# One run of attention slots over four batches, ahead of a 512-step GRU

## The chip, the core and the metric

The kernel runs on one core of one Trainium2 chip. A core has five engines that run side by side: TensorE (PE, matrix products; its weight loads are shown as PEld), VectorE (DVE), ScalarE (ACT), GpSimd (POOL) and SyncE (SP, which here only starts transfers). Each engine takes its instructions in the order in which they are written; semaphores tie the engines together. The metric is the time of one execution on the device, in microseconds (us). Everything is float32.

## The reference, cut to what is computed

`x` is 4 batches of 512 rows by 512 features; `cond` is 4 by 512; there are 16 heads of 32.

```python
scale, shift = split(cond @ W_emb + b_emb)
xn   = rms_norm(x, g_norm) * (1 + scale) + shift
q,k,v = split(xn @ W_qkv)                      # 16 heads of 32
q, k = rms_norm(q, g_q), rms_norm(k, g_k)
o    = softmax(q @ k.T * 32**-0.5) @ v
x    = x + (o + o @ W_out)                     # the attention layer, added to x
hs   = GRU(cond, x): 512 wide, started from cond, one step for each position
x    = x + hs
```

In the GRU `r = sigmoid(..)`, `z = sigmoid(..)`, `n = tanh(i_n + r*h_n)`, `h = (1-z)*n + z*h`. The scan runs over the 512 positions, each step for the four batches at once.

## The kernel before

The program has two parts in time. First comes attention, one batch after another, then the input side of the GRU is begun, and then 512 GRU steps follow, which wait for each other. The diff touches the first part alone, and the way from it to the second.

**A batch of attention** (`for b in range(B)`, on every engine, L193 to L433 and L546 to L733) has four stages on TensorE. (1) The row transposes: the normed rows `xr` (four banks of 4 transposes, L327) and the raw rows `xb` (another four, L331) are transposed. DVE and ACT bring them out of PSUM as `xnT` (scaled and shifted by `mod_b`, L551 and L678) and `xT` (L557). (2) A run of `N_SLOTS` = 23 slots. In slot `s` the projection of tile `n = s` (q, k and v of one group of 4 heads and 128 rows, L355, 4 matmuls) stands beside the transposes of the normed q and k of tile `i = s - 2` (`transpose_qk`, L342) and beside the attention of "quad" `m = s - LAG` (4 heads, 128 query rows). There are 16 tiles and 16 quads, and LAG is 6. So slots 0 to 5 have projections alone, slots 6 to 15 have both, slots 16 to 21 have quads alone, and slot 22 ends the last quad. (3) The output projection of the batch (L430, 16 matmuls of 512 columns), from all of `oT`, the attention output, and `wout`. (4) The next batch.

**A quad in a slot**: TensorE makes the scores of 4 heads (L378) in the banks SC; DVE takes the row maxima (`negmax`, L701); ACT takes the exponentials (`probs`, L583) with their sums; TensorE transposes them (L416, 16 transposes, back into SC); DVE copies two heads and ACT two (`probsT`, L705 and L588); in the next slot TensorE multiplies them with `v_sb` (L392, "PV") into bank PO. The reciprocal sums, spread over the heads (`rexp`, L715), are transposed in the next slot (L351), copied by ACT (`rT_sb`, L578), and after four quads DVE multiplies them onto PO, which gives one group of `oT` (L721).

**The norms of q and k**: ACT squares the projected tile (`sq`, L566), DVE sums (`qk_ss`, L693), POOL adds, takes the power and spreads it (L282, L284, L286: `norm_qk`), DVE multiplies (`qn`, L687), and TensorE transposes `qn` into bank PM, from which ACT copies to `qkT` (L572).

**The ends of a batch**: POOL adds `oT` onto `xT` in one instruction of 128x2048 (L294), DVE adds the output projection in four parts (L733) into `x1T`, and signals `x1_ready`. After the last batch POOL clears half of the tile `seeds` (L297), and then starts the transfer of the GRU weights `whh` (L299). These lie in the place of `wqkv`, so it may start only when the last projection is done. DVE clears the other half and copies a bias into all of it (L725, L727). TensorE waits for `whh` and `x1_ready`, opens six banks (L468), and makes the first input-side products (`gi_piece`, L443). These go through DVE, SP and HBM before ACT seeds the first step.

The order of the work is written out by hand: it is the order of the code on each engine. In a full slot TensorE runs `transpose_qk(i)` first, then the transpose of `rexp`, then the four scores.

Of the kernel before, what the change touches and what calls it, by code (L numbers as in the profile page):

```python
# [28 lines left out]
ALU = mybir.AluOpType  # L29
ACT = mybir.ActivationFunctionType  # L30
# [4 lines left out]
P = 128  # L35
# [3 lines left out]
KT = D // P  # L39
# [8 lines left out]
N_SLOTS = N_QUADS + LAG + 1  # L48
# [11 lines left out]
def attention_gru_kernel(nc, x, cond, W_emb, b_emb, g_norm, W_qkv, g_q, g_k, W_out,  # L60
                         W_ih, W_hh, b_ih, b_hh, out):
    with ExitStack() as ctx:  # L62
# [20 lines left out]
        mod_b = sb("mod_b", [P, 2 * KT])  # L83
# [10 lines left out]
        xT = sb("xT", [P, KT, T])  # L94
# [31 lines left out]
        with ExitStack() as attention_only:  # L126
# [4 lines left out]
            xnT = attention_only.enter_context(nc.sbuf_tensor("xnT", [P, KT, T], F32))  # L131
# [10 lines left out]
        pj = lambda n: SC[n] if n < 4 else PJ[n % 2]  # L142
        X_BANKS = (PO, PJ[0], PJ[1], PM)
# [8 lines left out]
            "ssq_done", "rstd_done", "modb_ready", "xr_ready", "xn_ps", "xnT_dve", "xnT_act", "x_ps",  # L152
# [93 lines left out]
        def _(pool):  # L246
# [30 lines left out]
            for b in range(B):  # L277

                for n in range(N_TILES):
                    n1 = (b * N_TILES + (n + 1))  # L280
                    await_on_pool(s["ss_done"], n1)
                    nc.gpsimd.tensor_scalar(qk_ms[:, n % 2], qk_ss[:, n % 2], DH * EPS, None, ALU.add).then_inc(s["qkms_done"], 1)  # L282
                    await_on_pool(s["qkms_done"], n1)
                    nc.gpsimd.tensor_tensor(qk_rs[:, n % 2], qk_ms[:, n % 2], half_neg[:], ALU.pow).then_inc(s["qkrs_done"], 1)  # L284
                    await_on_pool(s["qkrs_done"], n1)
# [3 lines left out]
                if b < B - 1:  # L289
                    rms_of_rows(b + 1)  # L290

                await_on_pool(s["oT_ready"], (b * G + (G + 1)))
                await_on_pool(s["xT_ready"], (b * KT + KT))
                nc.gpsimd.tensor_tensor(xT[:].rearrange("p k t -> p (k t)"), xT[:].rearrange("p k t -> p (k t)"),  # L294
                                        oT[:].rearrange("p k t -> p (k t)"), ALU.add).then_inc(s["ox_ready"], 1)

            nc.gpsimd.memset(seeds[:, RING // 2:RING, 0:2 * P], 0.0).then_inc(s["seeds_clear"], 1)  # L297
            await_on_pool(s["proj_done"], B * N_TILES)
            pool.dma_start(whh[:], W_hh.rearrange("(k p) n -> p k n", p=P)).then_inc(ld_whh, 16)  # L299

        @block.tensor
        def _(pe):
# [17 lines left out]
            for b in range(B):  # L320

                for c in range(KT):
                    pe.wait_ge(s["x1_ready"], (b * KT + (c + 1)))
# [5 lines left out]
                for c in range(KT):  # L329
                    for t in range(TT):  # L330
                        last = transpose(ps[:, X_BANKS[c], P * t:P * t + P], xb[:, t, P * c:P * c + P])  # L331
                    last.then_inc(s["x_ps"], 1)
                pe.wait_ge(ld_wqkv, 16)

                def transpose_qk(i):
                    if i == 0:
                        pe.wait_ge(s["xT_ready"], b * KT + KT)
                    else:
                        pe.wait_ge(s["qkT_ready"], b * N_TILES + i)
                    pe.wait_ge(s["qn_done"], b * N_TILES + i + 1)  # L340
                    for a in range(2):
                        last = transpose(ps[:, PM, P * a:P * a + P], qn[:, i % 2, P * a:P * a + P])  # L342
                    last.then_inc(s["tqk_done"], 1)

                for slot in range(N_SLOTS):
                    n, i, m = slot, slot - 2, slot - LAG

                    def transpose_rexp():

                        pe.wait_ge(s["rexp_done"], (b * N_QUADS + m))  # L350
                        transpose(ps[:, PJ[slot % 2], 3 * P:4 * P], rexp[:]).then_inc(s["rtr_done"], 1)  # L351

                    def project(k):
                        g, t = divmod(n, TT)
                        return nc.tensor.matmul(ps[:, pj(n), 0:3 * P], xnT[:, k, P * t:P * t + P],  # L355
                                                wqkv[:, k, :].rearrange("p (a g n) -> p a g n", a=3, g=G)[:, :, g, :],
                                                start=(k == 0), stop=(k == KT - 1))

                    if slot >= LAG and i < N_TILES:
                        transpose_qk(i)  # L360
                    if 0 <= m - 1 and (i < N_TILES or m == N_QUADS):
                        transpose_rexp()
                    if 0 <= m < N_QUADS:

                        g, q = divmod(m, TT)
                        if q == 0:
                            pe.wait_ge(s["qkT_ready"], (b * N_TILES + (TT * g + TT)))
                        for hh in range(4):

                            if m == 0:  # L370
                                pass
                            elif hh < 2:
                                pe.wait_ge(s["ptev_dve"], (b * (2 * N_QUADS) + (2 * m - 1 + hh)))
                            else:
                                pe.wait_ge(s["ptev_act"], (b * (2 * N_QUADS) + (2 * m - 3 + hh)))
# [470 lines left out]
```

## Time and profile before

| | us |
|---|---|
| median of 3 runs | 2276.47 (2275.55 to 2278.33) |
| profiled execution | 2284.52 |
| its span, first to last instruction | 2282.4 |
| TensorE busy | 2181.6 (96%) |
| VectorE busy | 1253.8 (55%) |
| ScalarE busy | 1153.2 (51%) |
| GpSimd busy | 202.6 (9%) |

The profiled execution is 8 us above the median, of which 2 us lie outside its span. The share of busy time of TensorE is 96%, but the attention part and the GRU part have different limits, so the stretches have to be read one by one: attention and the way to the GRU take the first 648.8 us, the 512 steps the other 1633.6 us. The chain of work that ended last names the line that the time goes through; the timelines show one slot as it runs.

### The profile page before, as it was taken

What the parts mean: (1) busy time and instruction counts of PE and PEld (TensorE: products, weight loads), DVE (VectorE), ACT (ScalarE), POOL (GpSimd) and SP (SyncE); (2) the same over time, 40 slices, a digit from 0 to 9 for tenths busy, and PEclk for the clock granted to TensorE, in tenths of its full rate; (3) what the DMA queues carried; (4) which work ended last, traced back from release to release, by engine and by line L of the source; (5) the groups of instructions that cost most, each with busy time, mean ns of one, the idle gap of its engine ahead of it and who ended that gap; (6) DMA issues with size and microseconds to landing.
All of it is one profiled execution on the core that took longest, in us unless ns stands there. A gap on an engine that the chain in (4) does not pass through costs nothing.

```text
span 2282.4 us, 129581 instructions
## 1 busy us (share of the span) xinstructions
PE 2181.6 (96%) x58384; PEld 1704.1 (75%) x58384; DVE 1253.8 (55%) x4464; ACT 1153.2 (51%) x4603; POOL 202.6 (9%) x223
## 2 busy tenths in 40 slices
PE   5999999999799999999999999999999999999998
PEld 3655656556478888888888888888888888888776
DVE  2664656646535555555555555555555555555554
ACT  2664746646334454544545454554545454554544
POOL 4314233143200000000000000000000000000000
PEclk9999999999999999999999999999999999999999
DMA  6000000000110000000000000000001000000000
GB/s 212 1 1 19 2 19 1 2 1 1 56 41 23 17 26 18 27 18 27 20 22 28 17 27 19 26 18 27 22 20 30 17 28 17 28 19 23 26 5 13
DMA packets 41081, 54.99 MB, mean 24 GB/s; under 512 B 9424, under 2 KB 34000, under 8 KB 40528
## 3 DMA queue, kind: packets, MB, share of 16 engines
q1 hardware_dynamic: 34112, 38.81, 5.4%
q8 instruction: 459, 7.52, 1.4%
q0 software_dynamic: 1584, 7.73, 0.9%
q10 hardware_dynamic: 4832, 0.15, 0.1%
q14 instruction: 94, 0.77, 0.1%
HBM read 29.90 MB, written 16.78 MB: 20 GB/s over the span
## 4 chain that ended last, share of the span: by engine, by line
PE 85%; DVE 5%; ACT 4%; POOL 2%; issue 2%; DMA 1%; POOLq 1%; ACTq 1%; SPq 0%; DVEq 0%
PE ps L457 56%; PE ps L304 8%; PE ps L443 7%; PE ps L355 5%; PE ps L378 4%; PE ps L392 2%; DVE znT L778 2%; PE ps L430 2%; ACT xb L624 2%; DVE xb L789 2%; ACT z_trip L621 2%; POOL qk_rs L284 1%; POOLq L62 1%; DMA wqkv<-in_L_cond_W_hh 0%; POOL norm_qk L286 0%
## 5 line engine op out<-in xcount | busy, mean ns | idle before, releaser
L457 PE MATMUL ps<-wqkv,xb 128*4 128x128 f32 x49152 | 1480.1, 273 | 40.7 <-DVE xb L789 29.2
L457 PEld LDWEIGHTS ps<-wqkv,xb 128*4 128x4 f32 x49152 | 1224.5, 87 | 280.1 <-DVE xb L789 227.9
L621 ACT ACTIVATE z_trip<-znT 128x8 f32<-128x8 f32 x1024 | 219.0, 214 | 369.5 <-DVE znT L778 369.5
L789 DVE TENSOR_TENSOR_SCAN xb<-z_trip,xb 128x24 f32<-128x24 f32 x1024 | 213.3, 208 | 291.7 <-ACT xb L624 291.7
L794 DVE STREAM_TRANSPOSE rT<-ps 128x128 f32<-128x128 f32 x512 | 162.2, 317 | 346.9 <-PE ps L457 346.9
L778 DVE STREAM_TRANSPOSE znT<-ps 128x128 f32<-128x128 f32 x1024 | 313.1, 306 | 67.7 <-PE ps L457 6.8
L615 ACT ACTIVATE r_pair<-rT 128x16 f32<-128x16 f32 x512 | 112.4, 219 | 436.9 <-DVE rT L794 436.9
L443 PE MATMUL ps<-wih,x1T 128*32 128x256 f32 (+1 forms) x4096 | 240.2, 328 | 0.0
L624 ACT ACTIVATE xb<-v_pair 128x16 f32<-128x16 f32 x1024 | 222.8, 218 | 12.6 <-DVE v_pair L783 0.7
L783 DVE TENSOR_TENSOR_SCAN v_pair<-r_pair,znT 128x16 f32<-128x16 f32 x1024 | 196.1, 192 | 35.6 <-DVE znT L778 0.8
L583 ACT ACTIVATE probs<-ps,negmax 128x512 f32<-128x512 f32 x256 | 172.7, 686 | 69.2 <-DVE negmax L701 69.2
L355 PE MATMUL ps<-wqkv,xnT 128*128 128x384 f32 x512 | 194.2, 500 | 0.0
L701 DVE TENSOR_REDUCE negmax<-ps 128x1 f32<-128x512 f32 x256 | 160.5, 684 | 58.2 <-PE ps L378 58.2
L599 ACT ACTIVATE ps<-seeds 128x256 f32<-128x256 f32 x512 | 188.3, 368 | 0.0
L304 PEld LDWEIGHTS ps<-ident,probs 128*128 128x128 f32 x1024 | 114.1, 141 | 63.2 <-ACT probs L583 47.6
L598 ACT ACTIVATE ps<-seeds 128x128 f32<-128x128 f32 x512 | 134.4, 263 | 51.1 <-DMA seeds<-gi_spill 51.1
L304 PE MATMUL ps<-ident,probs 128*128 128x128 f32 x1024 | 153.5, 281 | 4.9 <-ACT probs L583 4.2
L443 PEld LDWEIGHTS ps<-wih,x1T 128*32 128x32 f32 x4096 | 126.9, 111 | 8.3 <-issue 3.6
L355 PEld LDWEIGHTS ps<-wqkv,xnT 128*128 128x128 f32 x512 | 87.3, 192 | 44.3 <-issue 12.6
L284 POOL TENSOR_TENSOR qk_rs<-qk_ms,half_neg 128x8 f32<-128x8 f32 x64 | 106.6, 1666 | 12.1 <-POOL qk_ms L282 12.1
L693 DVE TENSOR_REDUCE qk_ss<-sq 128x8 f32<-128x256 f32 x64 | 26.9, 420 | 124.4 <-ACT sq L566 124.4
L378 PE MATMUL ps<-qkT 32*128 32x512 f32 x512 | 94.5, 663 | 0.0
(76 smaller groups left out, 985.6 us busy)
## 6 DMA issues: line engine op xcount, KB each, us to landing
gi_spill<-gi_image SPq DMA_DIRECT2D x64, 192.0 KB, 2.1
seeds<-gi_spill SPq DMA_DIRECT2D x228, 32.0 KB
seeds<-gi_spill SPq DMA_DIRECT2D x284, 16.0 KB
xb<-in_x SPq DMA_DIRECT2D x4, 1024.0 KB, 5.6
out<-xb SPq DMA_DIRECT2D x64, 64.0 KB, 2.1
wqkv<-in_L_cond_W_qkv SPq DMA_DIRECT2D x1, 3072.0 KB, 11.9
wih<-in_L_cond_W_ih POOLq DMA_DIRECT2D x1, 3072.0 KB, 14.7
wqkv<-in_L_cond_W_hh POOLq DMA_DIRECT2D x1, 3072.0 KB, 10.5
```

The lines of the kernel that those rows point to most:

```text
L304: return nc.tensor.transpose(dst, src, ident[:])
L355: return nc.tensor.matmul(ps[:, pj(n), 0:3 * P], xnT[:, k, P * t:P * t + P], wqkv[:, k, :].rearrange("p (a g n) -> p a g n", a=3, g=G)[:, ...
L378: nc.tensor.matmul(ps[:, SC[hh], :], qkT[head, g % 2, 0, P * q:P * q + P], qkT[head, g % 2, 1, :], start=True, stop=True, tile_position=(D ...
L443: last = nc.tensor.matmul(ps[QD * j:QD * j + QD, bank, first:first + width], x1T[:, k, b, BLK * block_no:BLK * block_no + BLK], gate_cols( ...
L457: last = nc.tensor.matmul(ps[QD * j:QD * j + B, bank, 0:P], hist_flat[:, first:first + 3 * B - 2:3], weights, start=False, stop=False, ski ...
L583: nc.scalar.activation(probs[:, hh, :], ps[:, SC[hh], :], ACT.Exp, bias=negmax[:, m % 2, hh:hh + 1], accum_out=sums[:, m % 2, hh:hh + 1]). ...
L599: nc.scalar.activation(ps[:, zna_bank:znb_bank + 1, 0:P].rearrange("p h (g n) -> p h g n", g=2), seeds[:, step % RING, P:3 * P].rearrange( ...
L621: nc.scalar.activation(z_trip[:, 8 * half:8 * half + 8, 2], znT[:, half, 0:16:2], ACT.Sigmoid).then_inc(s[z_name], 1)
L624: nc.scalar.activation(elements(step, half).rearrange("p (e s) -> p e s", s=3)[:, :, 0:3:2], v_pair[:, 8 * half:8 * half + 8, 1].unsqueeze ...
L778: return nc.vector.transpose(znT[:, half, :].rearrange("p (r k b s) -> p k r s b", r=4, k=4, b=B, s=2), ps[:, bank, 0:P])
L783: return nc.vector.tensor_tensor_scan(v_pair[:].rearrange("p e s -> p (e s)")[:, first:first + 16], r_pair[:].rearrange("p e s -> p (e s)" ...
L789: return nc.vector.tensor_tensor_scan(next_elements(step, half), z_trip[:].rearrange("p e s -> p (e s)")[:, 24 * half:24 * half + 24], ele ...
```

## The change

The slots of all four batches become one run: `N_SLOTS` is now 64 + 7 = 71, and tiles and quads are counted through all batches. A batch has no row transposes and no output projection of its own any more (but for the first batch's transposes and the last batch's output projection). They are cut into pieces, and a piece stands at the end of a slot on TensorE, in bank PM. `piece_of(slot)` says which: within the 16 slots of batch `b`, slots 2 to 5 transpose the raw rows of batch `b` ("x", `b` >= 1), slots 7 to 10 make the four parts of the output projection of batch `b - 1` ("y"), slots 11 to 14 transpose the normed rows of batch `b + 1` ("xn"). The piece is brought out of PM at the start of the next slot, by ACT or DVE; `transpose_qk`, which needs PM, waits for that (`await_piece`). `xT` and `xnT` have two places. `transpose_qk(i)` moves behind the four scores on TensorE, and ACT's copy of it behind that of `rT_sb`. The sums of squares of the next batch go to the ends of slots 7 and 8 on ACT, the normed rows to the ends of slots 9 and 10 on DVE, POOL's addition of `oT` is cut into one part for each group, and the transfer of `whh` is started by POOL in slot 65, ahead of the last additions and the clearing of `seeds`. The copy into `mod_b` is gone.

```diff
-N_SLOTS = N_QUADS + LAG + 1
+ALL_TILES = B * N_TILES
+ALL_QUADS = B * N_QUADS
+N_SLOTS = ALL_QUADS + LAG + 1
...
-        xT = sb("xT", [P, KT, T])
+        xT = sb("xT", [P, 2, KT, T])
...
+        X_SLOT, Y_SLOT, XN_SLOT = 2, 7, 11
+
+        def piece_of(slot):
+            b, u = divmod(slot, N_TILES)
+            if not 0 <= slot < ALL_TILES:
+                return None
+            if b >= 1 and X_SLOT <= u < X_SLOT + KT:
+                return "x", b, u - X_SLOT
+            if b >= 1 and Y_SLOT <= u < Y_SLOT + KT:
+                return "y", b - 1, u - Y_SLOT
+            if b < B - 1 and XN_SLOT <= u < XN_SLOT + KT:
+                return "xn", b + 1, u - XN_SLOT
+            return None
...
+                if 0 <= done < ALL_QUADS and done % TT == TT - 1:
+
+                    b, g = divmod(done // TT, G)
+                    await_on_pool(s["oT_ready"], b * G + g + 2)
+                    await_on_pool(s["xT_ready"], b * KT + KT)
+                    nc.gpsimd.tensor_tensor(xT[:, b % 2, g, :], xT[:, b % 2, g, :], oT[:, g, :], ALU.add).then_inc(s["ox_ready"], 1)
+                if slot == ALL_TILES + 1:
+                    await_on_pool(s["proj_done"], ALL_TILES)
+                    pool.dma_start(whh[:], W_hh.rearrange("(k p) n -> p k n", p=P)).then_inc(ld_whh, 16)
...
+            def run_piece(slot):
+                kind, b, c = piece_of(slot)
+                pe.wait_ge(s["qkT_ready"], slot - 1)
+                if kind == "x":
                     for t in range(TT):
-                        if c == 0:
-                            pe.wait_ge(s["xr_ready"], (b * TT + (t + 1)))
-                        last = transpose(ps[:, SC[c], P * t:P * t + P], xr[:, t, P * c:P * c + P])
+                        last = transpose(ps[:, PM, P * t:P * t + P], xb[:, t, P * c:P * c + P])
+                    last.then_inc(s["x_ps"], 1)
+                elif kind == "xn":
...
+                else:
+                    pe.wait_ge(ld_wout, 16)
+                    pe.wait_ge(s["oT_ready"], b * G + G + 1)
+                    out_projection(c, PM)
...
+                piece = piece_of(slot - 1)
+                if piece is not None:
+                    kind, b, c = piece
+                    if kind == "xn" and c % 2 == 0:
+                        scaled_rows(b, c, PM)
+                    elif kind == "y":
+                        residual(b, c, PM)
...
+                    if b > 0:
+                        dve.wait_ge(s["ox_ready"], b * KT)
+                        dve.wait_ge(s["y_done"], b * KT)
+                    nc.vector.tensor_tensor(oT[:, g, :], ps[:, PO, :], rT_sb[:, g % 2, :], ALU.mult).then_inc(s["oT_ready"], 1)
+                b, u = divmod(slot, N_TILES)
+                if b < B - 1 and u in (9, 10):
+                    over_rms(b + 1, (0, 1) if u == 9 else (2, 3))
```

TensorE, a full slot of the kernel before, from the transposes of q and k (`qn`) to the last two matmuls of the projection (`wqkv,xnT`):

```order
L304 MATMUL ps<-ident,qn 128x128 x2
L304 MATMUL ps<-ident,rexp 128x128
L378 MATMUL ps<-qkT 128x512 x4
L392 MATMUL ps<-probsT,v_sb 32x128 x16
L355 MATMUL ps<-wqkv,xnT 128x384
L304 MATMUL ps<-ident,probs 128x128 x8
L355 MATMUL ps<-wqkv,xnT 128x384
L304 MATMUL ps<-ident,probs 128x128 x8
L355 MATMUL ps<-wqkv,xnT 128x384 x2
```

TensorE, slot 23 of the changed kernel (slot 7 of its second batch), which ends with a part of the output projection:

```order
L320 MATMUL ps<-ident,rexp 128x128
L427 MATMUL ps<-qkT 128x512 x4
L320 MATMUL ps<-ident,qn 128x128 x2
L443 MATMUL ps<-probsT,v_sb 32x128 x16
L406 MATMUL ps<-wqkv,xnT 128x384
L320 MATMUL ps<-ident,probs 128x128 x8
L406 MATMUL ps<-wqkv,xnT 128x384
L320 MATMUL ps<-ident,probs 128x128 x8
L406 MATMUL ps<-wqkv,xnT 128x384 x2
L374 MATMUL ps<-oT,wout 128x512 x4
```

The two transposes of `qn` now stand between the scores and PV, and a quarter of what stood at the batch's end stands at the slot's end.

VectorE at the same point of the program, the end of slot 26 and the start of slot 27 of the changed kernel, where the last quarter of an output projection is brought out of PM (`x1T<-ps,xT`):

```order
L753 TENSOR_TENSOR qn<-ps,norm_qk 128x256
L788 COPY rexp<-recip 128x128
L798 TENSOR_TENSOR oT<-ps,rT_sb 128x512
L715 TENSOR_SCALAR xr<-xb,rstd 128x512 x2
L759 TENSOR_REDUCE qk_ss<-sq 128x8
L743 TENSOR_TENSOR x1T<-ps,xT 128x512
L774 TENSOR_REDUCE negmax<-ps 128x1 x4
```

The write to `oT` (L798) stands there behind a wait for all four quarters of the output projection, and ahead of two normed rows, a sum and the residual, all ahead of the next maxima.

GpSimd at the end of attention, before:

```order
L286 TENSOR_TENSOR norm_qk<-g_row,qk_rs 128x256
L294 TENSOR_TENSOR xT<-xT,oT 128x2048
L297 MEMSET seeds 128x18x256
L299 DMA wqkv<-in_L_cond_W_hh 128x4x1536
```

and in the changed kernel:

```order
L300 TENSOR_TENSOR norm_qk<-g_row,qk_rs 128x256
L313 DMA wqkv<-in_L_cond_W_hh 128x4x1536
L310 TENSOR_TENSOR xT<-xT,oT 128x512 x2
L315 MEMSET seeds 128x18x256
```

The transfer of the GRU weights now stands ahead of the last two additions and the clearing.

## Rows read from the trace of the kernel before

**Rows 1.** Busy time of each engine by stretch, with granted clock, DMA share, GB/s

```profile
58.28:122.30 64.02, 64.02 (x605) 41.14 (x604) 42.85 (x92) 43.81 (x126) 22.69 (x27) 1.00 0.01 2
560.80:598.97 38.17, 35.67 (x380) 20.28 (x379) 26.25 (x52) 27.03 (x71) 2.52 (x3) 1.00 0.01 2
612.95:624.84 11.89, 0.00 (x0) 0.03 (x1) 2.03 (x7) 0.00 (x0) 2.12 (x2) 0.66 0.70 265
624.84:648.83 23.99, 19.76 (x433) 13.23 (x434) 2.79 (x5) 0.73 (x4) 0.00 (x0) 0.86 0.17 50
648.83:2282.40 1633.57, 1591.00 (x53376) 1348.45 (x53376) 892.21 (x3739) 809.03 (x3647) 0.00 (x0) 1.00 0.07 22
...
624.84:631.70 6.86, 6.86 (x120) 4.30 (x124) 0.00 (x0) 0.00 (x0) 0.00 (x0) 0.60 0.01 2
631.70:642.00 10.30, 10.30 (x260) 7.28 (x256) 2.23 (x4) 0.00 (x0) 0.00 (x0) 1.00 0.22 80
```

**Rows 2.** Chain of work that ended last, at two batch ends: start, us, what

```profile
160.46 13.97 PE ps L430 x32
...
614.23 10.53 DMA wqkv<-in_L_cond_W_hh
```

**Rows 3.** Timeline of TensorE through one full slot: start, us, engine, line, operation

```profile
240.66 1.14 PE L378 MATMUL ps<-qkT 32*128 32x512 f32 x8
241.73 1.08 PE L392 MATMUL ps<-probsT,v_sb 128*32 128x128 f32 x32
242.75 0.91 PE L355 MATMUL ps<-wqkv,xnT 128*128 128x384 f32 x2
243.49 1.22 PE L304 MATMUL ps<-ident,probs 128*128 128x128 f32 x8
244.55 0.81 PE L355 MATMUL ps<-wqkv,xnT 128*128 128x384 f32 x2
245.19 1.04 PE L304 MATMUL ps<-ident,probs 128*128 128x128 f32 x8
246.07 1.46 PE L355 MATMUL ps<-wqkv,xnT 128*128 128x384 f32 x4
247.36 0.38 PE L304 MATMUL ps<-ident,qn 128*128 128x128 f32 x2
247.58 0.27 PE L304 MATMUL ps<-ident,rexp 128*128 128x128 f32 x1
247.78 1.14 PE L378 MATMUL ps<-qkT 32*128 32x512 f32 x8
```

**Rows 4.** Timelines of DVE (first row) and ACT in the same slot

```profile
241.82 2.49 DVE L701 TENSOR_REDUCE negmax<-ps 128x1 f32<-128x512 f32 x4 [0.38 <-PE ps L378]
...
242.55 0.69 ACT L583 ACTIVATE probs<-ps,negmax 128x512 f32<-128x512 f32 x1 [1.11 <-DVE negmax L701]
...
243.23 0.68 ACT L583 ACTIVATE probs<-ps,negmax 128x512 f32<-128x512 f32 x1
```

**Rows 5.** Timelines of DVE and TensorE in slot 6 of the first batch

```profile
49.48 0.42 DVE L687 TENSOR_TENSOR qn<-ps,norm_qk 128x256 f32<-128x256 f32 x1 [0.97 <-POOL norm_qk L286]
...
54.30 1.32 PE L304 MATMUL ps<-ident,probs 128*128 128x128 f32 x8 [0.35 <-ACT probs L583]
```

**Rows 6.** Groups of instructions: busy us, mean ns; and one stretch of DVE's timeline

```profile
L733 DVE TENSOR_TENSOR x1T<-ps,xT 128x512 f32<-128x512 f32 x16 | 10.6, 684 | 17.2 <-PE ps L430 12.8 <-POOL xT L294 4.4
L539 ACT ACTIVATE xr<-xb 128x512 f32<-128x512 f32 x16 | 9.8, 625 | 0.0
L678 DVE TENSOR_SCALAR xnT<-ps,mod_b 128x512 f32<-128x512 f32 x8 | 6.2, 806 | 2.0 <-PE ps L304 1.9
...
21.87 2.06 DVE L652 TENSOR_SCALAR xr<-xb,rstd 128x512 f32<-128x512 f32 x4 [7.88 <-POOL rstd L263]
```

**Rows 7.** Timeline of GpSimd: its addition in the first batch and in the last

```profile
162.56 4.51 POOL L294 TENSOR_TENSOR xT<-xT,oT 128x2048 f32<-128x2048 f32 x1
...
599.10 11.30 POOL L294 TENSOR_TENSOR xT<-xT,oT 128x2048 f32<-128x2048 f32 x1 [34.02 <-DVE oT L721]
```

More of the change, by code:

```diff
@@ new lines, in _ @@
+            for c in range(KT):
+                for t in range(TT):
+                    if c == 0:
+                        pe.wait_ge(s["xr_ready"], t + 1)
+                    last = transpose(ps[:, SC[c], P * t:P * t + P], xr[:, t, P * c:P * c + P])
+                last.then_inc(s["xn_ps"], 1)
+            for c in range(KT):
+                for t in range(TT):
+                    last = transpose(ps[:, X_BANKS[c], P * t:P * t + P], xb[:, t, P * c:P * c + P])
+                last.then_inc(s["x_ps"], 1)
@@ new lines, in transpose_qk, with out_projection @@
+            def transpose_qk(i):
+                if i == 0:
+                    pe.wait_ge(s["xT_ready"], KT)
+                else:
+                    pe.wait_ge(s["qkT_ready"], i)
+                await_piece(i + 1)
+                pe.wait_ge(s["qn_done"], i + 1)
+                for a in range(2):
+                    last = transpose(ps[:, PM, P * a:P * a + P], qn[:, i % 2, P * a:P * a + P])
+                last.then_inc(s["tqk_done"], 1)
+            def out_projection(c, bank):
+                for k in range(KT):
+                    last = nc.tensor.matmul(ps[:, bank, :], wout[:, k, P * c:P * c + P], oT[:, k, :],
+                                            start=(k == 0), stop=(k == KT - 1))
+                last.then_inc(s["y_done"], 1)
@@ L435, in _ @@
+            pe.wait_ge(s["oT_ready"], B * G + 1)
+            for c in range(KT):
+                out_projection(c, SC[c])
             pe.wait_ge(ld_wih, 16)
@@ L534, in _, with sum_squares @@
                 act.dma_start(g_row[:, 1, hh, :], g_k.partition_broadcast(P)).then_inc(ld_g, 16)
-            def sum_squares():
-                for t in range(TT):
+            def sum_squares(part):
+                for t in part:
                     last = nc.scalar.activation(xr[:, t, :], xb[:, t, :], ACT.Square, accum_out=ssq[:, t:t + 1])
-                last.then_inc(s["ssq_done"], 1)
+                if part[-1] == TT - 1:
+                    last.then_inc(s["ssq_done"], 1)
             act.wait_ge(ld_x, 16)
-            sum_squares()
+            sum_squares(range(TT))
@@ L644, in _, with over_rms @@
         def _(dve):
-            prime = (("x1_ready", KT), ("oT_ready", 1))
-            for name, count in prime:
-                dve.sem_inc(s[name], count)
-            def over_rms(batch):
+            dve.sem_inc(s["oT_ready"], 1)
+            def over_rms(batch, part):
                 dve.wait_ge(s["rstd_done"], (batch + 1))
-                for t in range(TT):
+                for t in part:
                     nc.vector.tensor_scalar(xr[:, t, :], xb[:, t, :], rstd[:, t:t + 1], None, ALU.mult).then_inc(s["xr_ready"], 1)
@@ L737, in _ @@
+            nc.vector.memset(seeds[:, 0:RING // 2, 0:2 * P], 0.0)
+            dve.wait_ge(ld_bias, 16 * 8)
+            nc.vector.tensor_copy(seeds[:, :, 2 * P:3 * P],
+                                  b_hid[:, 2 * P:3 * P].unsqueeze(1).broadcast_to([P, RING, P])
+                                  ).then_inc(s["seeds_clear"], 1)
+            for c in range(KT):
+                residual(B - 1, c, SC[c])
             dve.wait_ge(ld_bias, 16 * 8)
```

417 lines of the change are left out of this document (205 added, 212 removed).

## The prediction

> **What bounds the kernel now.** I read the stretches first. The GRU steps begin at 648.83 us and take 1633.57 us [rows 1]; no line of theirs changes. So the question is what becomes of the 648.83 us ahead of them. The chain of waits puts nearly all of them on TensorE and marks the batches: the first output projection starts at 160.46 us [rows 2], the last at 598.97 us (the end of a stretch in [rows 1]), three batches later, so a batch takes 146.2 us.
>
> Next, how fast a batch could be. Slots 7 to 15 of the first batch, where every kind of work is there, take 64.02 us, 7.11 us each, and TensorE is busy in all of it [rows 1]. Slots 16 to 22, with quads and no projections, take 38.17 us [rows 1], 5.45 us each, for clearly less TensorE work; those are bound by the way from scores to probabilities and back. The changed kernel fills three of the four emptying ends, and three of the four beginnings, with other batches' slots.
>
> Third, one full slot [rows 3]. The starts of its groups give what each takes: scores 1.07, PV 1.02, first projection 0.74, 8 transposes 1.06, projection 0.64, 8 transposes 0.88, two projections 1.29, `qn` 0.22, `rexp` 0.20, sum 7.12. The first projection and the first 8 transposes take 0.10 and 0.18 more than their twins: there TensorE waits. The wait is for this chain: scores start at 240.66, first maximum at 241.82, first exponential at 242.55, its transposes at 243.49 (2.83 after the scores), the second exponential 0.68 later [rows 3, 4]. TensorE's own work in between is 1.07 + 1.02 + 0.64 = 2.73, so it comes 0.1 too early, then 0.25 too early for the second head. Without waits the slot would be 6.84.
>
> **The change part by part.** I lay the new run along the time of the profiled execution.
>
> *Up to slot 7.* Before, slot 7 starts at 58.28 [rows 1]. In slot 6 the scores stood behind the transposes of tile 4; now they don't, but DVE writes `qn` of tile 4 (done at 49.90 [rows 5]) ahead of the first maximum. From there, maximum to exponential 0.73 and on to the transposes 0.94 [rows 4] gives 51.6 in place of 54.30 [rows 5]. Some of these 2.7 us may go to slow matmuls; I take 2.0: slot 7 at **56.3**.
>
> *57 full slots* (7 to 63). `transpose_qk` moves behind the scores, into the time in which TensorE waited. Its own work before the first transposes is now 2.73 + 0.22 = 2.95 against a chain of 2.83: no wait. For the second head the chain needs 3.51 and TensorE comes at 2.95 + 0.44 = 3.39: 0.12 left. So a slot is 6.84 + 0.12 = **6.95**, bounds 6.84 (no wait) and 7.11 (nothing gained). The new danger is ACT: its copy to `qkT` now waits for transposes that end about 1.45 after the scores' start and blocks it some 0.3, to 1.75 to 1.85; the exponential comes at 1.89 (242.55 - 240.66). It fits by less than 0.15. 57 x 6.95 = **396.2**.
>
> *The pieces.* 12 raw and 12 normed ones of 4 transposes, 0.44 each (half of 0.88 [rows 3]): 10.5. 12 quarters of the output projection, a quarter of 13.97 [rows 2] each, 3.49: 41.9. Sum **52.4**. This is work that was there before and is now moved.
>
> *Waits of the pieces.* A piece in PM must be out before the next `transpose_qk`, 1.27 us into the next slot (0.20 for `rexp` + 1.07). After an output projection everything else of DVE is long done: the residual (0.68 [rows 6]) is over by about 0.95. Nothing is lost. On ACT the raw rows come after two short copies and are over by 0.8: nothing. The normed rows on DVE (0.81 [rows 6]) stand behind the sum of squares and end at about 1.5: 0.2 each, six times, 1.2. The two sums of squares on ACT (0.63 each [rows 6]) have an output projection as cover in slots 7 and 8, but not in the first batch: 0.45 twice, 0.9. The costly place is slot 11 of batches 1 to 3. The write to `oT` waits on DVE for the last quarter, which ends 0.2 into slot 11. Behind it are queued itself 0.68, two normed rows 1.03 (half of 2.06 [rows 6]), a sum 0.4, the residual 0.68 and the maxima. PM is free at 3.0 in place of 1.27: 1.7 for batches 1 and 2, 0.7 for batch 3, in all 4.1. Sum **6**. Bounds: 0, or 0.7 us for each of 36 pieces, 25, if an evacuation is never covered.
>
> *The tail.* Slots 64 to 70 as before, 38.17 [rows 1], less 0.2 for each of two slots with the new order: **37.8**. The last output projection: **14.0** [rows 2].
>
> *From attention to the GRU.* Before, TensorE is idle for 11.89 us from 612.95 [rows 1], until the transfer of `whh` (10.53, started at 614.23 [rows 2]) has landed. It had to wait for POOL's addition and clearing. Now it is started in slot 65, some 45 us ahead. What is late next is the last residual: **0.8**. (POOL's last addition, a quarter of 4.51 [rows 7], may be stretched by DVE's clearing as the last one was, to 11.30 [rows 7]; the 14.0 of the output projection cover it.)
> From there 23.99 us to the first step [rows 1]. Of these the first 6.86 us have matmuls alone, at a mean granted clock of 0.60, and the next ones have 1.00 [rows 1]. At 1.00 the first would take 6.86 x 0.60 = 4.1. TensorE doesn't idle before them now, so I take 24.0 - 2.8 = **21.2**, bounds 21.2 and 24.0.
> *The GRU*: **1633.6**.
>
> **Sum**: 56.3 + 396.2 + 52.4 + 6 + 37.8 + 14.0 + 0.8 + 21.2 + 1633.6 = 2218.4, against a span of 2282.4: 64.0 us less. The profiled execution is 8 us above the median of the runs; I take the same saving from the median: 2276.5 - 64.0 = **2212.5**.
>
> The row on the clock is the place where a rule matters. The full slots have waits of 0.1 to 0.2 us and a granted clock of 1.00 throughout, and so have the tails, with 2.5 us idle in 38.2 [rows 1]. The Trainium skill, page "TensorE: Matmul & The Clock Gate", section "A second HAM failure mode: psum-queue depth-cycling", says that short idle spells between groups of matmuls that go round PSUM banks can make the gate swing between its levels. By it, the many more waits on bank PM could cost more than the waits themselves; the trace speaks against it, since the slots with such waits stay at full clock. Its price would be that of the clock rival below.
>
> **The rivals.**
> *The slot is not shorter (7.11 or a little more).* ACT's copy to `qkT` stands in front of the exponential with less than 0.15 us to spare; where that is used up, what the new order gave is lost. 57 x 0.16 = 9 us: 2222. Against it: the copies on ACT are short and their inputs early.
> *The pieces wait at bank PM.* Each of 36 evacuations costs 0.7 us: 25 in place of 6: 2232. For it: DVE and ACT each have a chain into the exponentials with no slack at the second head. Against: after an output projection both are idle.
> *`whh` or the clock gives nothing back.* The transfer lands in time only if POOL gets to slot 65 with the others; if the start of the GRU is held by something else, for instance the spill and fetch of input products, 11 + 2.8 us stay: 2226.
> *All waits vanish.* 57 x 0.12 + 6 = 13: 2200.
> *Slower than before: the granted clock falls in the merged run.* Place: the slots with pieces. Price: a full slot of 6.84 us of TensorE work takes about that much longer at 1.2 GHz. The gain of 64.0 is gone after 9.4 such slots of 57; with 20 of them the time is 2349. For it: granted clock 0.60 and 0.66 where TensorE has stood still for 12 us [rows 1]. Against: no full slot of the trace shows it.
>
> **How the numbers follow.** Forecast 0.58; slot not shorter 0.16; pieces wait 0.10; nothing back at the GRU's start 0.06; all waits vanish 0.05; clock falls 0.03; the rest 0.02, on either side. The range takes in the low bound of the unknown costs (2200) and the two dearer cases (2222 and 2232) with some room: 2200 to 2234. About 0.2% (4.6 us) is what a measurement tells from no change; every case but the clock and the rest is far below that: faster 0.95, same 0.01, slower 0.04.
>
> **What would show it.** Right: the spacing of scores in a full slot at 6.95; slots 7 to 10 of batches 1 to 3 at 10.4; slots 27 and 43 longer by 1.7, with TensorE released by `x1T`; the output projection's last start near 549 and the first GRU step near 585; the idle time before the bank opening under 1 us. Wrong: maxima or exponentials as releasers of more than 0.3 us a slot; a granted clock under 1.00 between 60 and 560 us; a GRU part other than 1633 us.

## The result, and the profile after

The changed kernel takes 2219.18 us (median of 4, 2216.73 to 2220.65) where the kernel before takes 2276.81 (median of 4, 2275.55 to 2278.33): ratio 0.9746, interval 0.9729 to 0.9762. That is 57.6 us less; 64.0 were forecast, and 2212.5 us. The range (2200 to 2234) holds the time. The profiled execution has a span of 2218.3 us against 2218.4 in the sum, but this agreement is an accident, as the terms show: the way to the first GRU matmul came out 7.7 us too short in the sum and the GRU part 7.7 us too long. Four executions of the sets below took 2437.6, 5047.0, 7657.4 and 12334.3 us, far above all others, and stand in no median here.

The stretches of the changed kernel, which answer to [rows 1] (start and end; us; busy us of PE, PEld, DVE, ACT and POOL with their instructions; granted clock; DMA share; GB/s):

```profile
60.00:515.00 455.00, 449.92 (x3952) 285.38 (x3950) 289.57 (x607) 294.66 (x830) 161.55 (x189) 1.00 0.02 6
570.07:571.00 0.93, 0.00 (x0) 0.03 (x1) 0.84 (x2) 0.00 (x0) 0.00 (x0) 1.00 0.00 0
571.00:592.38 21.38, 17.09 (x432) 12.93 (x433) 3.98 (x11) 0.72 (x4) 0.00 (x0) 0.98 0.18 56
592.38:2218.30 1625.92, 1584.95 (x53376) 1344.25 (x53376) 891.63 (x3739) 807.51 (x3647) 0.00 (x0) 1.00 0.08 22
```

Between 60 and 515 us TensorE is idle for 5.1 of 455 us, at a granted clock of 1.00. The idle time ahead of the bank opening is 0.93 us where it was 11.89 [rows 1], and the way from there to the first GRU matmul 21.38 where it was 23.99. The first GRU matmul starts at 592.38, 56.45 earlier than before.

One full slot of it on TensorE (slot 8), as in [rows 3]:

```profile
63.87 0.27 PE L320 MATMUL ps<-ident,rexp 128*128 128x128 f32 x1
64.07 1.14 PE L427 MATMUL ps<-qkT 32*128 32x512 f32 x8
65.14 0.44 PE L320 MATMUL ps<-ident,qn 128*128 128x128 f32 x2
65.51 1.08 PE L443 MATMUL ps<-probsT,v_sb 128*32 128x128 f32 x32
66.52 0.91 PE L406 MATMUL ps<-wqkv,xnT 128*128 128x384 f32 x2
67.27 1.05 PE L320 MATMUL ps<-ident,probs 128*128 128x128 f32 x8
68.16 0.81 PE L406 MATMUL ps<-wqkv,xnT 128*128 128x384 f32 x2
68.80 1.04 PE L320 MATMUL ps<-ident,probs 128*128 128x128 f32 x8
69.68 1.46 PE L406 MATMUL ps<-wqkv,xnT 128*128 128x384 f32 x4
70.97 0.27 PE L320 MATMUL ps<-ident,rexp 128*128 128x128 f32 x1
```

The slot is 70.97 - 63.87 = 7.10 us, and the slots without a piece take 7.09 to 7.11: as good as the 7.11 before, and not the 6.95 of the sum. Read the differences of the starts. The first eight transposes of `probs` take 0.89 (67.27 to 68.16), not 1.06 as in [rows 3]: that wait is gone, as forecast. But the two transposes of `qn` take 0.37 (65.14 to 65.51) where they took 0.22 [rows 3], and the first projection matmul still takes 0.75 although nothing is waited for.

Slot 27, where the write to `oT` stood behind the last part of an output projection, on TensorE and then on DVE:

```profile
212.96 3.60 PE L374 MATMUL ps<-oT,wout 128*128 128x512 f32 x8
216.39 0.27 PE L320 MATMUL ps<-ident,rexp 128*128 128x128 f32 x1
216.59 1.14 PE L427 MATMUL ps<-qkT 32*128 32x512 f32 x8
219.20 0.41 PE L320 MATMUL ps<-ident,qn 128*128 128x128 f32 x2 [1.47 <-issue]
...
216.69 0.69 DVE L798 TENSOR_TENSOR oT<-ps,rT_sb 128x512 f32<-128x512 f32 x1 [4.97 <-PE ps L374]
217.30 0.87 DVE L715 TENSOR_SCALAR xr<-xb,rstd 128x512 f32<-128x512 f32 x2
218.09 0.41 DVE L759 TENSOR_REDUCE qk_ss<-sq 128x8 f32<-128x256 f32 x1
218.42 0.68 DVE L743 TENSOR_TENSOR x1T<-ps,xT 128x512 f32<-128x512 f32 x1
```

DVE stands still for 4.97 us until the output projection ends, and then runs through the queue that was forecast: `oT`, two normed rows, a sum, the residual. The residual ends at 219.1, and the transposes of `qn` start at 219.20. The profile puts the 1.47 us down to "issue"; the DVE rows beside it show what was waited for.

### The profile page after: what moved, and what is told of

It is laid out like the page before. It is cut to its first block, busy times and chain, and to the rows that moved or that the text cites. A ratio compares the mean times of both kernels' runs of the same rounds, so it can differ in the third digit from the quotient of the medians.

```text
span 2218.3 us, 129719 instructions
## 1 busy us (share of the span) xinstructions
PE 2141.1 (97%) x58384; PEld 1693.7 (76%) x58384; DVE 1239.9 (56%) x4460; ACT 1150.6 (52%) x4603; POOL 204.8 (9%) x235
## 4 chain that ended last, share of the span: by engine, by line
PE 88%; DVE 5%; ACT 4%; issue 2%; ACTq 1%; POOL 1%; DMA 0%; SPq 0%; POOLq 0%; DVEq 0%
PE ps L502 58%; PE ps L320 7%; PE ps L406 7%; PE ps L488 7%; PE ps L427 3%; PE ps L443 3%; DVE znT L851 3%; PE ps L374 2%; ACT xb L689 2%; DVE xb L862 2%; ACT z_trip L686 2%; POOL qk_rs L298 0%; ACTq L575 0%; DMA seeds<-gi_spill 0%; ACTq L576 0%
## 5 line engine op out<-in xcount | busy, mean ns | idle before, releaser
L488 PE MATMUL ps<-wih,x1T 128*32 128x256 f32 (+1 forms) x4096 | 235.7, 326 | 0.0
L406 PE MATMUL ps<-wqkv,xnT 128*128 128x384 f32 x512 | 200.5, 498 | 0.0
L320 PEld LDWEIGHTS ps<-ident,probs 128*128 128x128 f32 x1024 | 118.6, 141 | 43.6 <-issue 21.3
L320 PE MATMUL ps<-ident,probs 128*128 128x128 f32 x1024 | 136.3, 274 | 1.0 <-ACT probs L648 0.7
L406 PEld LDWEIGHTS ps<-wqkv,xnT 128*128 128x128 f32 x512 | 83.1, 190 | 32.0 <-issue 11.3
L653 ACT ACTIVATE probsT<-ps 128x512 f32<-128x512 f32 x128 | 70.1, 595 | 40.9 <-PE ps L320 40.0
```

The lines of the kernel that those rows point to most:

```text
L320: return nc.tensor.transpose(dst, src, ident[:])
L406: return nc.tensor.matmul(ps[:, pj(n), 0:3 * P], xnT[:, b % 2, k, P * t:P * t + P], wqkv[:, k, :].rearrange("p (a g n) -> p a g n", a=3, g ...
L488: last = nc.tensor.matmul(ps[QD * j:QD * j + QD, bank, first:first + width], x1T[:, k, b, BLK * block_no:BLK * block_no + BLK], gate_cols( ...
```

## The experiments

A kernel's attention part is compared by the start of its first GRU matmul. It repeats within 0.1 us in two profiled executions of the changed kernel (592.38 and 592.41). In four of the kernel before it lies at 648.83, 648.51, 648.96 and 645.86, so what is compared with that kernel is known to some 3 us only. Medians are compared within one set of runs, on one chip: the kernel before took 2276.8, 2283.0, 2278.0, 2290.6 and 2279.6 us in five sets, of which the second and the third were on the same chip.

**The old place of the transposes of q and k.**

```diff
+                if slot >= LAG and i < ALL_TILES:
+                    transpose_qk(i)
                 if 0 <= m - 1 and (i < ALL_TILES or m == ALL_QUADS):
                     transpose_rexp()
...
-                if slot >= LAG and i < ALL_TILES:
-                    transpose_qk(i)
                 if 0 <= m - 1 < ALL_QUADS:
```

(and the same on ACT with `evacuate_qk`, ahead of the copy to `rT_sb`)

> The changed kernel with the transposes of q and k back ahead of the rexp transpose and the scores on TensorE, and ACT's copy of them ahead of that of rT_sb, as before; all else as changed. Theory: what the new order is worth is the cover of the pieces, since bank PM must now be free at the start of a slot and not 1.27 us into it. Full slots without a piece go from 7.09 to 7.11 us; the slot after a piece waits 0.8 to 1.0 us (raw rows, residual, normed rows on ACT), 1.5 us (normed rows on DVE), 2.6 us in slots 27 and 43: 36 pieces, about 40 us in place of the 5 us of the changed kernel. First GRU matmul at about 628 in place of 592.4, median about 2255. Rival (the order matters little, evacuations are quick enough): first GRU matmul under 600, median 2220 to 2227.

Measured: 2266.5 us, ratio to the kernel before 0.9926 (0.9906 to 0.9947); first GRU matmul at 635.49. A slot after an output projection on TensorE:

```profile
192.34 3.60 PE L374 MATMUL ps<-oT,wout 128*128 128x512 f32 x8
196.84 0.41 PE L320 MATMUL ps<-ident,qn 128*128 128x128 f32 x2 [0.90 <-issue]
197.08 0.27 PE L320 MATMUL ps<-ident,rexp 128*128 128x128 f32 x1
```

From start to start of the scores, slots without a piece take 7.11 us, those with raw rows 8.48, with an output projection 11.64, with normed rows 8.66 or 9.17. Less the pieces' own 0.43 and 3.43 that is a wait of 0.93, 1.10, 1.12 and 1.63, and 2.8 in slots 27 and 43: 45 us over the 36 pieces, against 5.1 in the changed kernel. With 2.0 us more up to slot 7 this is the 43.1 us by which the GRU starts later. The theory holds, with 635.5 where about 628 was expected: the waits are each some 0.1 larger than I had them, slots 27, 43 and 59 more, and the 2.0 us ahead of slot 7 I had not counted. So of the 56 us of the change, 43 hang on the place of two transposes, and not because a slot gets shorter by it: it is the 1.27 us that the evacuations of bank PM have. What is left of the saving here, 648.8 - 635.5 = 13.3 us, is what the early transfer of `whh` gives by itself (13.6 to 14.2, below). With the transposes at their old place, one run in place of four gains nothing that these runs can tell.

**The transposes of q and k beside other whole-array work.** Each slot has a place for them where their neighbours are 128x128 too.

```diff
                         pe.wait_ge(s["r_ready"], m)
                     project(0)
+                if slot >= LAG and i < ALL_TILES:
+                    transpose_qk(i)
```

(taken out from behind the scores; ACT's `evacuate_qk` goes behind its four exponentials)

> The changed kernel with the transposes of q and k placed after the first projection matmul of a slot, next to the transposes of probs, and ACT's copy of them after the four exponentials. In the changed kernel two of these 128x128 transposes stand between scores (tiles of 32 rows) and PV (tiles of 32 columns) and take 0.37 us where they took 0.22 next to the rexp transpose. Theory: the 0.15 is a price of changing between tiled and whole-array matmuls twice more; beside other whole-array matmuls it goes, so a full slot is 6.92 to 6.95 us in place of 7.09: 57 x 0.15 = 9 us; the waits for PM in slots 27 and 43 (1.5 each) and after the normed rows on DVE go as well, about 5 us. First GRU matmul at about 578, median about 2205. Rival (7.09 us is what TensorE needs for this work in any order, the 0.37 is the time of loading qn): slot 7.09, only the 5 us of waits go, median about 2214.

Measured: 2212.6 us, ratio 0.9688 (0.9670 to 0.9706); first GRU matmul at 581.06, 11.3 us earlier than in the changed kernel.

```profile
120.95 1.14 PE L427 MATMUL ps<-qkT 32*128 32x512 f32 x8
122.02 1.08 PE L441 MATMUL ps<-probsT,v_sb 128*32 128x128 f32 x32
123.03 0.91 PE L406 MATMUL ps<-wqkv,xnT 128*128 128x384 f32 x2
123.78 0.38 PE L320 MATMUL ps<-ident,qn 128*128 128x128 f32 x2
124.00 1.04 PE L320 MATMUL ps<-ident,probs 128*128 128x128 f32 x8
...
215.59 0.38 PE L320 MATMUL ps<-ident,qn 128*128 128x128 f32 x2
216.72 1.32 PE L320 MATMUL ps<-ident,probs 128*128 128x128 f32 x8 [0.76 <-ACT probs L646]
```

The two transposes take 0.22 again (123.78 to 124.00), the first projection keeps its 0.75, and the slot is 6.94 (the next scores start at 127.89). Only slots 8 and 9 keep 7.11; the other 55 are shorter by 0.15 or 0.16, which makes some 8.5 us. I had expected the wait in slots 27 and 43 to go as well; the last row shows that it only changed its place. DVE gets to the maxima late there, so the exponentials are late, and TensorE waits for `probs`: slots 27 and 43 are 1.2 us longer than their like and slot 59 is 0.4 longer, so 3 us of the forecast 14 were not there.

**A second way to make the same two changes of tiling.** Here the one transpose of `rexp` goes from ahead of the scores to between scores and PV, in the kernel just shown.

```diff
-                if 0 <= m - 1 and (i < ALL_TILES or m == ALL_QUADS):
+                if 0 <= m - 1 and m == ALL_QUADS:
                     transpose_rexp()
...
+                    if 0 <= m - 1 and i < ALL_TILES:
+                        transpose_rexp()
```

> The kernel with the transposes of q and k after the first projection matmul, and the one transpose of rexp moved from ahead of the scores to between scores and PV. Theory (a change between whole-array and tiled matmuls costs 0.07 to 0.1 us wherever it is made, and two more are made here): full slot 7.05 to 7.10 in place of 6.94. Rival (the 0.37 us of the changed kernel belongs to the transposes of qn, their weights or their wait, not to the place): full slot 6.94 again.

Measured: one execution, 2220.5 us; first GRU matmul at 588.96, 7.9 later than without this edit.

```profile
122.21 1.14 PE L427 MATMUL ps<-qkT 32*128 32x512 f32 x8
123.28 0.33 PE L320 MATMUL ps<-ident,rexp 128*128 128x128 f32 x1
123.54 1.08 PE L443 MATMUL ps<-probsT,v_sb 128*32 128x128 f32 x32
...
127.92 1.46 PE L406 MATMUL ps<-wqkv,xnT 128*128 128x384 f32 x4
129.30 1.14 PE L427 MATMUL ps<-qkT 32*128 32x512 f32 x8
```

The slot is 7.09 us (122.21 to 129.30), for 6.94 of the same slot without this edit. The transpose takes 0.26 between the two. At its old place it took 0.11: from the last projections to the scores it is 1.38 here (127.92 to 129.30), and it was 1.49 with the transpose in between (126.40 to 127.89). A transpose among others takes 0.11 too (8 in 0.88). So the price goes with the place, not with `qn`: a piece of whole-array work between the scores (32 rows) and PV (32 columns) costs 0.15 us more than elsewhere.

**The transfer of the GRU weights alone**, in the kernel before:

```diff
                 if b < B - 1:
                     rms_of_rows(b + 1)
+                else:
+                    await_on_pool(s["proj_done"], B * N_TILES)
+                    pool.dma_start(whh[:], W_hh.rearrange("(k p) n -> p k n", p=P)).then_inc(ld_whh, 16)
...
-            await_on_pool(s["proj_done"], B * N_TILES)
-            pool.dma_start(whh[:], W_hh.rearrange("(k p) n -> p k n", p=P)).then_inc(ld_whh, 16)
```

> The kernel before, with the transfer of W_hh started by POOL after the last norm of the last batch, ahead of its last addition and the clearing of seeds; nothing else. Theory: TensorE's idle 11.9 us before the opening of the banks shrinks to the wait for the last residual, 0.9, and since the engine has not stood still, the first input-side matmuls run at a granted clock of 1.00, which gives 2.8 more: the stretch from the end of the last output projection to the first GRU matmul goes from 35.9 to 22.2, the median from 2276.8 to 2263. Rival (the clock's share is not due to the idle time): 11 us only, clock again near 0.6 in the first 7 us, 2266. Rival (the clearing of seeds or the additions hold the start): under 5 us.

Measured: 2266.2 us, ratio 0.9926 (0.9907 to 0.9944), 16.8 less than the kernel before in the same set. Timeline of POOL, then of TensorE:

```profile
598.54 11.29 POOL L297 TENSOR_TENSOR xT<-xT,oT 128x2048 f32<-128x2048 f32 x1 [33.24 <-DVE oT L722]
...
613.25 1.49 PE L469 MATMUL ps<-ident 128*4 128x128 f32 x48 [0.88 <-DVE x1T L734]
```

and the stretches behind, columns as above:

```profile
613.25:634.62 21.37, 17.09 (x432) 12.85 (x433) 3.98 (x11) 0.73 (x4) 0.45 (x1) 1.00 0.18 57
...
613.25:617.00 3.75, 3.75 (x108) 3.08 (x112) 1.19 (x6) 0.00 (x0) 0.45 (x1) 1.00 0.02 4
```

The bank opening starts at 613.25 in place of 624.84, and its first stretch has a granted clock of 1.00 where it had 0.60 [rows 1]: from there to the first GRU matmul 21.37 in place of 23.99. POOL's addition is as long as it was (11.29, [rows 7]), and costs nothing, since the 14 us of the output projection cover it. First GRU matmul at 634.62, 14.2 earlier, of which 0.6 lie ahead of the last output projection, which no edit touches. So 13.6 to 14.2 of the 56.45 us of the change come from this edit, which has nothing to do with merging the batches.

**The output projection one slot earlier.**

```diff
-        X_SLOT, Y_SLOT, XN_SLOT = 2, 7, 11
+        X_SLOT, Y_SLOT, XN_SLOT = 2, 6, 11
```

> The changed kernel with the parts of the output projection in slots 6 to 9 of a batch in place of 7 to 10, so that the write to oT at the end of slot 10 does not wait for the last of them. Theory: the wait of 1.47 us in slots 27 and 43 and its smaller one in slot 59 go, 3.7 us in all: first GRU matmul at about 588.7, median about 2215.5. Rival: the wait only moves. In slot 6 the output projection needs the oT that DVE writes at the very end of that slot, and two normed rows at the end of slot 10 lose their cover: nothing gained or up to 2 us lost.

Measured: first GRU matmul at 588.64, 3.74 earlier, as worked out; 2218.7 us, ratio 0.9722 (0.9700 to 0.9744). Against the changed kernel's 0.9746 (0.9729 to 0.9762) the medians alone would not show it. The wait did not only move: of 5.1 us of idle time between 60 and 515 us 1.5 are left, in six places of 0.24, behind the normed rows on DVE.

**Both edits.** First the changed kernel itself, on the same chip:

> The changed kernel itself, once more, as the standard for the runs beside it. Theory (the GRU part is the same in all of these kernels and its length differs from execution to execution): first GRU matmul at 592.4 again, within 0.3 us, and a GRU part somewhere from 1625 to 1634 us, so a span of 2217 to 2226. Rival (the change itself makes the GRU part 7 us shorter than the 1633.6 of the kernel before): 1626 again, and the kernel before never near that.

Measured: 2223.6 us, ratio 0.9756 (0.9740 to 0.9772), first GRU matmul at 592.41, GRU part 1629.4. Then the kernel with the late transposes and `Y_SLOT = 6`:

> Both edits: transposes of q and k after the first projection matmul, and the output projection's parts in slots 6 to 9. With the transposes alone moved, slots 27 and 43 were still 1.2 us longer than their like (released by probs), since DVE gets to the maxima late behind the write to oT, two normed rows and the residual. Theory: with the write to oT no longer waiting, these go: 3 us off 581.1, first GRU matmul at about 578, median 3 us below that of the transposes alone (2212.6), so about 2209 and 10 below the changed kernel beside it. Rival (the lateness comes from the two normed rows themselves, wherever the output projection stands): no gain, first GRU matmul at 581.

Measured: 2207.2 us, ratio to the kernel before 0.9687 (0.9674 to 0.9699), and 16.4 us below the changed kernel beside it. First GRU matmul at 577.00, 15.4 earlier than the changed kernel's and 4.1 earlier than with the transposes alone, where 3 were expected.

```profile
60.00:500.00 440.00, 440.00 (x3944) 285.34 (x3943) 288.64 (x604) 290.20 (x827) 160.80 (x187) 1.00 0.02 6
```

TensorE has no idle time left between 60 and 500 us. This kernel beats both.

**The length of the GRU part.** It is the same code in all of these kernels, and its length, from the first GRU matmul to the end, was 1633.6 us in the kernel before and 1625.9 in the changed one. Four more runs bear on whether the change has to do with it.

> The kernel before, once more, for the length of its GRU part. In the profiled execution shown first it took 1633.6 us from the first GRU matmul; in all kernels with the changed ends it took 1625.9 to 1629.7. Theory (it differs from execution to execution, with the code the same): first GRU matmul at 648.8 again, within 0.3 us, and a GRU part of 1625 to 1633, most likely near 1629. Rival (the late transfer of W_hh or the order before makes the GRU part longer): 1633 or more again.

> The kernel before, a third time, for the same question: theory 648.8 and 1625 to 1633 us, differing from the run beside it by some us; rival 1633 or more again.

Measured: 1641.2 and 1637.5 us (spans 2289.7 and 2286.5), on the chip on which the kernel before is slowest, with the first GRU matmul at 648.5 and 649.0. By themselves these speak for the rival. So the kernel before and the one with the early transfer were run on one chip:

> The kernel before beside the one with the early transfer of W_hh, on one chip, for the length of the GRU part, which was 1633.6, 1641.2 and 1637.5 us in three profiled executions of the kernel before and 1625.9 to 1629.7 in seven of kernels with an early transfer, on other chips. Theory (it goes with the chip and the moment): on one chip the two have GRU parts within 3 us of each other, and their medians differ by the 14.2 us ahead of the first GRU matmul, 12 to 17. Rival (the late transfer makes the GRU part longer): the GRU part is 6 us or more longer here than in the run beside it, and the medians differ by 20 or more.

> The other half of that pair: the kernel before with the early transfer of W_hh. Theory: first GRU matmul at 634.6, GRU part within 3 us of that of the kernel before beside it. Rival: GRU part near 1628 while that of the kernel before is 1634 or more.

Measured: GRU parts of 1631.7 (first matmul at 645.86) and 1626.8 (at 634.36), 4.9 apart, which neither theory had; medians 2278.4 and 2268.0, 10.4 apart, ratio of the latter to the kernel before 0.9954 (0.9934 to 0.9974). Profiled executions of the kernel before have the longer GRU parts, 4 of 4 (1631.7 and more, the nine others 1625.9 to 1629.7). The medians don't settle it: here they differ by 10.4 us, in the earlier pair by 16.8, for 11.5 and 14.2 us ahead of the first GRU matmul; for the changed kernel the difference was 57.6 and then 54.4, for 56.4; and for the old place, the late place, `Y_SLOT = 6` and both edits it was 16.5, 70.4, 64.3 and 70.8, for 13.3, 67.8, 60.2 and 71.8.

What the records show is where the time lies: most steps take 3.14 us, and 64 to 93 steps in the four executions of the kernel before took over 3.2, against 38 to 53 in the others. In such a step TensorE stands still with "issue" as the reason. What the long steps take over 3.145 us each adds up to 16.0 us in the kernel before and 8.0 in the changed one, which makes up the 7.7 between the two. The very first step is a matter of the clock:

```profile
592.38:598.38 6.00, 6.00 (x160) 4.63 (x164) 2.09 (x8) 3.19 (x10) 0.00 (x0) 0.77 0.35 99
...
592.41:598.40 5.99, 5.99 (x108) 4.11 (x112) 1.55 (x6) 2.55 (x8) 0.00 (x0) 0.50 0.35 99
```

These are the first 6 us of the GRU part in two executions of the changed kernel, after 4.3 us in which TensorE had nothing to do. The granted clock is 0.77 in one and 0.50 in the other, and by the second step the other is 1.5 us late, of the 3.5 by which their GRU parts differ. Beside that, 18 steps are long in all six executions of the kernel before and of the one with the early transfer (105, 166, 215 and 227 among them), and 13 steps, none of them the same, in all seven of the changed kernel and its variants (91, 201, 262 and 311 among them). So some long steps go with the program; but the early transfer has the same 18 and a short GRU part. What holds TensorE in the long steps stays open.

## Why the prediction came out as it did

| term of the sum | forecast | measured |
|---|---|---|
| slot 7 starts at | 56.3 | 56.8 |
| 57 full slots | 396.2 | 404.4 (7.095 each) |
| the pieces' own work | 52.4 | 51.6 (24 x 0.43, 12 x 3.44) |
| waits of the pieces | 6 | 5.1 |
| slots 64 to 70 | 37.8 | 38.0 |
| last output projection | 14.0 | 14.0 |
| wait for the last residual | 0.8 | 0.9 |
| to the first GRU matmul | 21.2 | 21.4 |
| GRU | 1633.6 | 1625.9 |

(The measured terms add up to the span within 0.2 us.)

*What bounds the kernel* was right: TensorE in the full slots, and the emptying ends and beginnings of the batches as the time to be had. Without the end (13.9) and the shorter slot (9.1) the forecast saving of 64.0 is 41.0 us; measured, it is 56.45 less 13.6 less 1.0, which is 41.9.

One thing in the saving the prediction doesn't name. The kernel before also lost time to the clock at the beginning of its batches. TensorE at the start of slot 6 of the second batch, and a stretch behind it:

```profile
196.63 0.49 PE L304 MATMUL ps<-ident,qn 128*128 128x128 f32 x2 [2.34 <-DVE qn L687]
...
196.80:200.20 3.40, 3.40 (x12) 1.02 (x10) 1.05 (x2) 0.70 (x2) 1.89 (x2) 0.50 0.00 0
```

TensorE waited 2.34 us for `qn`, and the granted clock was then 0.50 for a while; so it was at the same place of the third and the fourth batch. In the four executions of the kernel before, and the two with the early transfer, the time from one output projection to the next is 145.4 us in the 6 batches without such a stretch and 146.0 to 146.4 in 11 with one; one batch has a longer stretch, and 147.5. By these, some 2.4 us of the saving (146.41 + 146.15 + 145.96 - 3 x 145.37) are an estimate of what the clock gave back; and how many such stretches an execution has moves its first GRU matmul, between 645.86 and 648.96. The changed kernel has one such beginning, and from 50 to 515 us a granted clock of 1.00 in the execution shown.

*The step that failed* is "*57 full slots*": "Its own work before the first transposes is now 2.73 + 0.22 = 2.95". The 0.22 was read where the transposes stood beside another whole-array transpose. Between scores and PV they take 0.37. And the 0.10 by which the first projection is longer than its twin was read as a wait; it is there in every kernel, also where TensorE waits for nothing, so it belongs to the change from PV to whole-array work. Of the 0.28 us called waits only 0.18 was one. The new order took that away and gave 0.15 back. This is the time that the rival "the slot is not shorter" gives (7.11), but not its mechanism: ACT's copy, which it blamed, held nothing. The late and the between experiments show the price in both directions (6.94 and 7.09). On ACT the same slot shows what released the first exponential:

```profile
65.62 0.38 ACT L632 ACTIVATE qkT<-ps 128x256 f32<-128x256 f32 x1 [0.38 <-PE ps L320]
66.16 0.69 ACT L648 ACTIVATE probs<-ps,negmax 128x512 f32<-128x512 f32 x1 [0.16 <-DVE negmax L774]
```

The copy was over, and ACT stood for 0.16 us until DVE's maximum was there. The exponential ends at 66.85, before TensorE comes to its transposes at 67.27.

*The pieces and their waits* came out term by term: the raw rows and the residual cost nothing, the normed rows on DVE 0.24 to 0.29 where 0.2 was forecast, slots 27 and 43 1.5 where 1.7 was. The sums of squares in the first batch, for which 0.9 was put down, cost nothing.

*The end* was right in both its parts, the 11 us of the transfer and the 2.6 of the clock, and the experiment with this edit alone has each of them.

*The GRU part* was taken from a profiled execution that was 8 us above the median, and the saving was carried over to the median as it stood. This was sound for the median: 57.6 us were saved, and 56.45 lie ahead of the GRU. Only the agreement of the two spans must not be read as precision, and a GRU part other than 1633 us stood in the prediction's own list of what would show it wrong.

*The clock rival* is out: 1.00 in all the full slots. The swings of the clock that the Trainium skill (page "TensorE: Matmul & The Clock Gate", section "A second HAM failure mode: psum-queue depth-cycling") tells of for idle spells between groups of matmuls did not come at waits of this size: with 36 evacuations of one bank, and in the first experiment with 45 us of waits behind them, the granted clock between 56 and 515 us stayed at 1.00. In the kernel before the clock did fall to 0.50 at most of the batch beginnings, behind a wait of 2.34 us, and in the first experiment a wait of 2.65 us in slots 27 and 43 changed nothing; what makes the difference is not shown.

## What to carry to other kernels

When a loop of short pipelined slots is bound by one engine, the gain lies in never letting it run empty: join the runs, and hang the work between them on the slots in pieces, each with a place for its evacuation that the engine reaches a microsecond later. Here that place was what made the joining pay: without it one run of 71 slots was no faster than four of 23. Before you count a difference between two twins in a timeline as a wait, look for the same difference where nothing can be waited for; a price that goes with the neighbours moves along with the instruction. And look at what is queued ahead of the transfer that the next phase waits for: here 14 us lay there, free for the moving of one line.

## What the runs showed of the hardware

Small whole-array matmuls between two kinds of tiled ones (rows, then columns) cost 0.15 us more on TensorE than beside whole-array ones: 0.37 against 0.22 for two transposes, 0.25 or 0.26 against 0.11 for one, and the slot moves by 0.15 or 0.16 with each. After PV the first whole-array matmul takes 0.10 longer than its like in all kernels.

POOL's addition of 128x2048 takes 4.51 us in the first batch and 11.3 in the last, while DVE clears and fills another tile [rows 7]; a quarter of it takes 1.25 us in the slots of the changed kernel and 8.06 at the same place of the end, as these rows of POOL and then of DVE show:

```profile
536.35 1.25 POOL L310 TENSOR_TENSOR xT<-xT,oT 128x512 f32<-128x512 f32 x1 [13.23 <-DVE oT L798]
556.27 8.06 POOL L310 TENSOR_TENSOR xT<-xT,oT 128x512 f32<-128x512 f32 x1 [18.67 <-DVE oT L798]
...
556.91 3.90 DVE L802 MEMSET seeds<- 128x4608 f32 x1 [0.91 <-issue]
560.72 2.50 DVE L804 COPY seeds<-b_hid 128x4608 f32<-128x4608 f32 x1
```

The 6.8 us more are the same for a quarter of the work, so POOL is held for as long as DVE runs, not slowed in proportion: DVE's copy ends at 563.22 and POOL's addition 1.1 us later. In the first batch of the kernel before it is DVE that is held. POOL's addition starts at 162.56 [rows 7], and this row of DVE starts just behind it:

```profile
162.62 5.92 DVE L652 TENSOR_SCALAR xr<-xb,rstd 128x512 f32<-128x512 f32 x4 [2.31 <-POOL rstd L263]
```

The same four took 2.06 us at 21.87 [rows 6]. By the Trainium skill, page "SBUF — State Buffer", section "🔬 SBUF: two separate sides", the one of the two engines that starts first has their common ports for a whole instruction and the other is blocked, where DVE's instruction is in a 2-port mode or reads two inputs from SBUF. The traces agree that one of them is held, and in the first batch also on which. At the end they differ from it: POOL's recorded start is 0.64 us ahead of DVE's clearing and yet POOL is held, and it is held through the clearing, which reads no tile (by itself the addition would have been over at 557.5, and the copy starts at 560.72). Why is not shown.
